# Two chained cross-attentions: part of one subtraction moves from GpSimd to VectorE in step 6

## What is computed

```python
normed = x * rsqrt(mean(x * x, -1) + 1e-6) * norm_w
q, k, v = heads(normed @ wq), heads(ctx @ wk), heads(ctx @ wv)   # 16 heads of 64
attn = softmax(einsum('bhqd,bhkd->bhqk', q, k))
x = x + (einsum('bhqk,bhkd->bhqd', attn, v)) @ wo                # heads joined
w = softmax(einsum('brd,bfd->brf', x, ctx))
out = x + einsum('brf,bfd->brd', w, ctx)
```

## Time and profile before

| | |
|---|---|
| median of 3 runs | 588.2 us (587.67 to 589.69) |
| the profiled execution | 588.1 us, of which the span of its instructions is 586.4 us |
| PE busy | 568.3 us, 97% |
| PEld busy | 514.2 us, 88% |
| DVE busy | 454.7 us, 78% |
| ACT busy | 393.5 us, 67% |
| POOL busy | 456.6 us, 78% |
| L566 on POOL | 109 instructions, 338.9 us |
| L571 on POOL | 16 instructions, 1536 to 1855 ns each |

### The profile page before, as it was taken

One profiled execution on the slowest core, in us unless ns is written; L12 is line 12 of the kernel. 1 busy time (PEld: TensorE's weight loads), 2 busy tenths in 40 slices (PEclk: granted clock), 3 DMA queues, 4 the chain that ended last, 5 costly groups with the idle time before them and its releaser, 6 DMA issues.

```text
span 586.4 us, 10901 instructions
## 1 busy us (share of the span) xinstructions
PE 568.3 (97%) x3781; PEld 514.2 (88%) x3781; DVE 454.7 (78%) x641; ACT 393.5 (67%) x517; POOL 456.6 (78%) x532
## 2 busy tenths in 40 slices
PE   7999999999999999999999999999999999999997
PEld 7878888898999889999999899898899888988885
DVE  5778699679886988879886898868887788868504
ACT  5677667758675876757766677757768476756803
POOL 3337785997789887987879897997789977999810
PEclk9999999999999999999999999999999999999999
DMA  7066847766566667666567766666666765656400
GB/s 224 1 161 161 206 128 177 184 173 156 151 176 173 193 155 186 167 189 155 148 175 180 190 169 158 180 186 150 158 176 175 196 163 155 179 146 177 120 1 8
DMA packets 47808, 92.45 MB, mean 158 GB/s; under 512 B 14698, under 2 KB 20234, under 8 KB 47754
## 3 DMA queue, kind: packets, MB, share of 16 engines
q1 hardware_dynamic: 39834, 76.71, 51.9%
q10 hardware_dynamic: 7920, 15.05, 9.5%
HBM read 8.72 MB, written 0.41 MB: 16 GB/s over the span
## 4 chain that ended last, share of the span: by engine, by line
PE 71%; DVE 8%; ACT 5%; POOL 5%; issue 5%; SPq 4%; DMA 1%; ACTq 1%
PE ps_o L1238 30%; PE ps_s L1117 9%; PE ps_s L1121 9%; PE ps_s L1118 9%; DVE neg_max L912 5%; PE ps_m L1161 4%; SPq L469 4%; POOL turned_p L566 3%; PE ps_m L1015 3%; ACT probs L715 2%; PE ps_o L1234 2%; DVE o_norm L886 1%; PE ps_m L1034 1%; ACT o_part L756 1%; DMA x_rows<-in_x_dram 1%
## 5 line engine op out<-in xcount | busy, mean ns | idle before, releaser
L566 POOL TENSOR_TENSOR turned_p<-turned_p 128x1408 fp32r<-128x1408 f32 (+1 forms) x109 | 338.9, 3110 | 10.3 <-ACT turned_p L744 9.4
L715 ACT ACTIVATE probs<-ps_s,neg_max 128x1444 f32<-128x1444 f32 (+1 forms) x109 | 160.0, 1468 | 135.0 <-DVE neg_max L912 129.3
L1238 PE MATMUL ps_o<-turned_p,c_hi 128*128 128x256 f32 (+2 forms) x1273 | 248.8, 291 | 1.7 <-DVE o_norm L886 1.7
L912 DVE TENSOR_REDUCE neg_max<-ps_s 128x1 f32<-128x1444 f32 (+1 forms) x111 | 184.1, 1659 | 64.5 <-PE ps_s L1121 64.0
L1238 PEld LDWEIGHTS ps_o<-turned_p,c_hi 128*128 128x128 f32 x1273 | 206.4, 189 | 3.8 <-issue 3.1
L1238 PE MATMUL ps_o<-turned_p,c_lo 128*128 128x256 f32 (+2 forms) x693 | 185.4, 270 | 0.0
L935 DVE STREAM_TRANSPOSE blocks<-probs 128x1408 f32<-128x1408 f32 (+1 forms) x109 | 178.1, 1634 | 0.8 <-issue 0.6
L744 ACT ACTIVATE turned_p<-turned_p 128x1536 fp32r<-128x1536 f32 (+1 forms) x109 | 156.4, 1435 | 4.6 <-DMA turned_p<-blocks 4.6
L1238 PEld LDWEIGHTS ps_o<-turned_p,c_lo 128*128 128x128 f32 x693 | 131.3, 189 | 0.0
L1117 PE MATMUL ps_s<-cT_hi,q_hi 128*128 128x512 f32 (+3 forms) x312 | 121.4, 389 | 1.1 <-DVE q_lo L813 1.1
L1121 PE MATMUL ps_s<-cT_hi,q_lo 128*128 128x512 f32 (+3 forms) x312 | 118.8, 381 | 0.0
(11 more groups left out here) (150 smaller groups left out, 450.9 us busy)
## 6 DMA issues: line engine op xcount, KB each, us to landing
turned_p<-blocks SPq DMA_DIRECT2D x667, 96.0 KB, 2.2
turned_p<-blocks ACTq DMA_DIRECT2D x141, 96.0 KB, 2.6
ctx_raw<-in_ctx_dram SPq DMA_DIRECT2D x8, 704.0 KB
turned_p<-blocks SPq DMA_DIRECT2D x40, 48.0 KB, 2.0
turned_p<-blocks ACTq DMA_DIRECT2D x24, 48.0 KB, 2.1
wq_sb<-in_L_xattn_wq_dram SPq DMA_DIRECT2D x2, 256.0 KB, 5.4
wk_sb<-in_L_xattn_wk_dram SPq DMA_DIRECT2D x2, 256.0 KB, 5.6
wv_sb<-in_L_xattn_wv_dram SPq DMA_DIRECT2D x1, 512.0 KB, 6.8
```

The source lines that it names most:

```text
L566: pool.tensor_tensor(lo, lo.bitcast(F32), hi.bitcast(F32), ALU.subtract).then_inc(remainder, 1)
L715: act.activation(probs[step % 2][0:m, 0:S], score_tile(step, m), ACT.Exp, bias=neg_max[0:m, s:s + 1], accum_out=sums[0:m, s:s + 1]).then_i ...
L912: dve.tensor_reduce(neg_max[0:m, s:s + 1], score_tile(step, m), AX.X, ALU.max, negate=True).then_inc(maxed, 1)
L1238: t = pe.matmul(*todo[i], start=(i == 0), stop=(i == len(todo) - 1))
```

## The change

For batch elements 1 to 7 the second part of the context's remainder (slots 6 to 10, 128x640) is no longer made on POOL at the start of step 6. DVE makes it, in its own step 6, between the maximum (with bank A) and the transposes. DVE gets a wait for ScalarE's `c_hi`; the subtraction, its operands and the semaphore that it raises are the same. The first part, and both parts of element 0, stay on POOL.

```diff
@@ GpSimd, for step in range(TOTAL)
-                if s in LO_STEPS and 1 <= b < B:
-                    ctx_lo(b, LO_STEPS.index(s))
+                if s == LO_STEPS[0] and 1 <= b < B:
+                    ctx_lo(b, 0)
                 take_remainder(*group_at(step, LO_LAG))
@@ VectorE
+            def ctx_lo(b):
+
+                j0, j1 = SPLIT_SLOTS[1]
+                dve.wait_ge(c_hi_done, 2 * b + 2)
+                dve.tensor_tensor(c_lo[b % 2][:, j0:j1, :], ctx_raw[:, j0:j1, :],
+                                  c_hi[b % 2][:, j0:j1, :].bitcast(F32), ALU.subtract).then_inc(c_lo_done, 1)
@@ VectorE, for step in range(TOTAL)
                 maximum(step)
                 read_bank(step, "A")
+                if s == LO_STEPS[1] and 1 <= b < B:
+                    ctx_lo(b)
                 if step - 1 in BY_PE[0:2]:
```

## The result

The changed kernel takes 597.04 us (median of 5 runs, 596.0 to 600.08) against 588.86 us for the kernel before (median of 5, 587.67 to 590.29): a ratio of 1.0149, 95% interval 1.012 to 1.0179. The forecast was 596.3 us. The profiled execution took 596.0 us, with a span of 594.2 us.

A forecast was written before the change was run, and what follows sets the result against it. PE was taken to bound the kernel, with DVE's o_norm on its path; 8.35 us of holds at seven sites less 0.26 us gave net 8.1 us on 588.1, 596.2, and 596.3 us as median, range 590.9 to 601.0 us.

The forecast's parts named there:

- What bounds the kernel: PE, busy 97% of the span; its L1161 waits for DVE's o_norm, 2.1 us, put DVE's step 6 on the path.
- The moved instruction's own price: DVE's step 6: 0.83 us for the subtraction, queue pushed by 0.75 us, slack 0.23 us, 1.10 us in element 1.
- the rival without contention: DVE's step 6: only its own price beyond slack counts, net 2.8 us, giving 591.0 us; chance 0.13.
- The hold: DVE's subtraction is blocked until POOL's running L566 ends; DVE goes on 0.60 us after that end; chance 0.66.
- The sum: At L1161, o_norm comes 1.03 to 1.43 us later in elements 1 to 7: 8.35 us, net 8.1 us.
- What comes back: Element 1's weight load at L1234 loses its 0.26 us wait for POOL; nothing is won in the other elements.
- The third rival: Later PE waits at L1234 and L1238 give the loss back: no slower, or faster, 587.6 or 584 us; chance 0.12.
- The rival in which POOL keeps its turn: DVE enters only after POOL's instructions behind L566: 600.6 us, chance 0.07, or after the next L566: 623 us, chance 0.02.
- What is hidden: Step 7's maximum, SyncE's spread DMAs and the context load slip without cost; uncovered, SyncE's 0.6 us would cost 4 us.
- the things that would make the forecast fail: POOL's phase shifting at step 6, or longer waits, 2.5 us in element 1, lowering the granted clock.

The follow-up runs named there:

- e3: Kernel before without POOL's second part of the remainder in elements 2 to 7, nothing in its place on DVE; 588.33 us, ratio 0.9995.
- e6: As the change, but DVE makes the part at the end of its step 6, behind the transposes and o_norm; 587.75 us, ratio 0.9987.
- e7: As the change, but DVE makes the part in step 7, behind the maximum, where it stood idle; 588.42 us, ratio 0.9989.
- e1: Kernel before plus an unused DVE tensor_reduce of 128x640, one SBUF operand, at the moved instruction's place; POOL keeps its part; 591.54 us, ratio 1.0037.
- e2: Kernel before with the subtraction made on DVE as in the change and again by POOL at its old place; 599.15 us, ratio 1.0168.
- e4: As the change, but DVE makes one slot (128x128) and POOL keeps four of the five; 592.49 us, ratio 1.0059.
- e5: As the change, but POOL's L566 of step 5 in elements 1 to 7 is cut into four instructions; 593.87 us, ratio 1.0081.
- e9: As the change, but PE fills its wait ahead of the output projection with transposes that nobody reads; 595.9 us, ratio 1.0116.

## Why the prediction was right

- **What bounds the kernel.** Right. The projection's wait for `o_norm` was the one place where the change reached PE; e3 shows that POOL's load was not, and e6 and e7 that DVE's load as such was not.
- **The moved instruction's own price**, 0.75 us a site with 0.23 us of slack. Right to 0.02 us, as far as e1's reduction stands for it: 0.73 us. Alone it gives e1's 591.54 us, the time that the rival without contention had (591.0).
- **The hold.** This was the term with the least behind it, one meeting of 0.45 us in the earlier trace rows against one of 0.36 us in the earlier trace rows. DVE went on 0.60 to 0.61 us after L566's end at every one of the seven sites of the change, and at the 21 others of its repetitions and e2; 0.07 us after it with 128 elements. 0.60 us was the forecast, and 0.07 us that of e4. The record of element 4 lasted 1.53 us ("about 1.5").
- **The sum.** 8.35 us at the sites; 8.11 by the lags of PE, 8.1 by the waits. The small difference is the site of element 3 (0.97 instead of 1.08) and 0.02 or 0.03 us at most others, where the record of `o_norm` is a little shorter (0.38 us against 0.42).
- **What comes back.** 0.31 us in element 1 for the forecast 0.26, nothing elsewhere that can be put down to the change. The third rival, that later waits would give the loss back, is wrong in the main: PE's waits at L1247 for `o_norm` are 1.7 us as before, they move with PE. Those at L1243 (L1234 before) fell from 1.7 to 0.8 us, though (1.0 and 1.4 us in the two repetitions), where I had said that all of them move with PE. Nearly all of that fall is the one wait at 480.68, of which the last point tells.
- **The rival in which POOL keeps its turn** is wrong: in every case DVE was served before POOL's next instruction, and POOL's tail copies waited (0.97 us for two).
- **What is hidden.** SyncE's spread DMAs, the maximum of step 7 and the context load cost nothing, as forecast: PE's lag stays flat between the sites, but for the places named in the section on the result.
- **What the sum leaves out.** The level of 596.3 us came from adding to an execution of the kernel before; the like execution of the change is 594.9 us, and its median of 597.04 is higher because the clock falls in some executions. I had named this among the things that would make the forecast fail, without a term for it. It adds about 2 us to the median of the change and about 0.8 us to that of the kernel before. Like for like, in executions with a mean granted clock of 0.999 or more, the change costs 7.0 us (588.05 to 595.0). That is 1.1 us less than the net 8.1 us of the sum, and the falls bring the difference of the medians to 8.2 us. The price of the hold was forecast; that the median came within 0.7 us of 596.3 is in part luck.
- **The level that it starts from.** Most of the 1.1 us is the wait of 0.86 us at 480.68 in the profile of before (1.03 us of PE's lag). It came from ScalarE, whose queue and PE's in the kernel before show it (the view puts two issues together; the second, at 475.9, took 2.25 us, where the median of that line is 0.52). The exponential and `o_part` came late behind it:

```profile
475.35 2.79 ACTq L735 DMA_DIRECT2D turned_p<-blocks  x2
478.25 1.47 ACT L715 ACTIVATE probs<-ps_s,neg_max 128x1444 f32<-128x1444 f32 x1 [2.31 <-issue]
479.70 0.37 ACT L756 ACTIVATE o_part<-ps_o 128x256 f32<-128x256 f32 x1
...
480.68 0.36 PE L1234 MATMUL ps_o<-turned_p,rinv_ones 128*128 128x256 f32 x1 [0.86 <-DVE o_norm L886]
```

That wait came in none of the three profiles of the change, but in e1's (0.81 us) and in part in e3's (0.26 us). Whether most executions of the kernel before have it, and whether the change removes it, is open. I had counted the 588.1 us as typical without asking which of its waits come every time.

What the runs show of the hold in the terms of the Trainium skill, "SBUF — State Buffer", section "Who interferes with whom": it says that a DVE instruction with two SBUF inputs contends with a GpSimd instruction that reads SBUF, while a tensor_reduce doesn't, and that the second one to come is blocked completely. The trace agrees on each of these: 1.31 to 2.73 us for L919 in the change, 0.81 us for e1's reduction, and POOL's copies held in turn. For the moment of release the page's 115 ns after the holder's end (another pair, another section of that page) is not what is seen here: DVE goes on 0.60 us after L566's recorded end with 0.73 to 0.75 us of its own to do, so it begins about 0.14 us before that end.

## What to carry to other kernels

Moving work from a loaded GpSimd to a VectorE with idle time isn't priced by the two durations. Where both would read two tiles of SBUF at once, VectorE waits for the rest of the GpSimd instruction that is running, so look in the trace at what GpSimd is in the middle of when VectorE arrives, and add that rest; a smaller piece pays it too (a fifth of the elements cost 4.4 of the 8.1 us of waits). Then place the instruction by what is queued behind it: the same instruction cost 8 us ahead of the result that TensorE waits for, and nothing behind it, even with twice the hold.

## What I had not expected of the hardware

- In one of the three profiles of the change the granted clock was at its lower level from 11.5 to 14.8 us, at the start of the kernel, with PE busy all through; the other two and the kernel before had none there. It cost 1.70 us of PE's lag. It isn't the change's: e3, e4 and e5 have it in the same stretch (0.50 or 0.51), and e1, e2, e7 and e9 each have a fall near the end, between 572 and 588 us. Comparing two traces span by span would have put that on the change.
- In e2 the clock fell inside the wait of 2.54 us in front of the projection and stayed at the lower level for 6.7 us; at the same wait in three profiles of the change it didn't. What decides is open.
- As a holder, POOL's tensor_scalar (0.60 us) in the earlier trace rows let DVE begin about 0.39 us before its record ended (371.76 + 0.36 - 0.227 = 371.89 against 372.28), where L566 does so about 0.14 us before. The same record of 0.36 or 0.37 us is at this place in every trace but that of e1; whether it is the instruction's kind or its length was not tried.
